# Clipped mixture of experts: the weighted sum moved from VectorE to ScalarE and GpSimd, the gate's product folded into silu

## The reference, cut to what matters

```python
def _swiglu(h):
    x_glu = jnp.minimum(h[..., ::2], LIMIT)              # LIMIT = 7.0
    x_lin = jnp.clip(h[..., 1::2], -LIMIT, LIMIT)
    return x_glu * jax.nn.sigmoid(ALPHA * x_glu) * (x_lin + 1.0)   # ALPHA = 1.702
...
logits = t @ gate_w + gate_b
top_v, top_i = jax.lax.top_k(logits, K)                  # K = 2
probs = jax.nn.softmax(top_v, axis=-1)
...
def body(acc, ew):
    w1, b1, w2, b2, we = ew
    h = _swiglu(t @ w1 + b1)
    y = h @ w2 + b2
    return (acc + we[:, None] * y, None)
```

## Time and profile before

| | us |
|---|---|
| median of 3 runs (lowest, highest) | 4638.23 (4637.52, 4643.8) |
| the profiled execution, its own time | 4647.3 |
| its span in the trace | 4644.3 |
| this sublayer in the trace, first VectorE instruction to the next sublayer's first matmul | 1157.0 to 1558.5 |
| TensorE busy over the span | 3836.4 (83%) |
| VectorE | 2840.3 (61%) |
| ScalarE | 2070.5 (45%) |
| GpSimd | 1152.7 (25%) |

### The profile page before, as it was taken

One profiled execution on the slowest core, in us unless ns is written; L12 is line 12 of the kernel. 1 busy time (PEld: TensorE's weight loads), 2 busy tenths in 40 slices (PEclk: granted clock), 3 DMA queues, 4 the chain that ended last, 5 costly groups with the idle time before them and its releaser, 6 DMA issues. The chain is left out here.

```text
span 4644.3 us, 84590 instructions
## 1 busy us (share of the span) xinstructions
PE 3836.4 (83%) x33378; PEld 2574.5 (55%) x33378; DVE 2840.3 (61%) x7587; ACT 2070.5 (45%) x3471; POOL 1152.7 (25%) x783
## 2 busy tenths in 40 slices
PE   0688888887999879898999996555359999598999
PEld 0466666566556556664555554435237776465665
DVE  9576777656899657666565655892452222476555
ACT  4466666544333225555554544430134444354332
POOL 3444444222444221003445452320000000010000
PEclk9999999999999769899999997776679999798999
DMA  2222222000000010000000000004100000000000
GB/s 92 47 47 47 50 48 48 17 1 1 1 1 1 1 51 2 2 1 1 2 2 2 2 2 1 21 21 153 59 14 1 1 1 1 28 2 2 1 10 10
DMA packets 58286, 92.04 MB, mean 20 GB/s; under 512 B 15922, under 2 KB 42501, under 8 KB 56133
## 3 DMA queue, kind: packets, MB, share of 16 engines
q1 hardware_dynamic: 53620, 79.83, 7.4%
q10 hardware_dynamic: 4272, 6.81, 0.4%
HBM read 42.43 MB, written 10.62 MB: 11 GB/s over the span
## 5 line engine op out<-in xcount | busy, mean ns | idle before, releaser
L853 PE MATMUL banks<-XT,weight_region 128*128 128x512 f32 x1696 | 781.2, 599 | 2.2 <-DVE T L1229 2.2
L875 PEld LDWEIGHTS banks<-weight_region,HT 128*128 128x128 f32 x4672 | 560.2, 192 | 151.4 <-issue 91.3
L1252 DVE SCALAR_TENSOR_TENSOR x_res<-banks,WT,x_res 128x128 f32<-128x128 f32 x1056 | 297.1, 344 | 488.7 <-PE banks L875 449.0
L875 PE MATMUL banks<-weight_region,HT 128*128 128x128 f32 x4672 | 569.6, 276 | 21.6 <-DVE HT L1240 15.3
L853 PEld LDWEIGHTS banks<-XT,weight_region 128*128 128x128 f32 x1696 | 305.8, 193 | 288.2 <-issue 283.2
L1005 ACT ACTIVATE HT<-banks,weight_region 128x512 f32<-128x512 f32 x256 | 173.4, 688 | 239.1 <-PE banks L853 232.9
L1068 POOL TENSOR_TENSOR FNM<-FNM,FRS 128x8 f32<-128x8 f32 x16 | 4.6, 288 | 1045.1 <-ACT FRS L964 1045.1
L458 DVE TENSOR_REDUCE MX<-banks 128x8 f32<-128x1152 f32 x128 | 173.2, 1353 | 116.0 <-PE banks L275 113.8
L384 ACT COPY PT<-banks 128x384 f32<-128x384 f32 x384 | 171.6, 481 | 132.1 <-PE banks L285 130.4
L1643 ACT COPY PT<-banks 77x512 f32<-77x512 f32 x256 | 143.3, 582 | 195.3 <-PE banks L1565 195.3
L1096 POOL TENSOR_TENSOR T<-T,T 128x512 f32<-128x512 f32 x128 | 162.8, 1273 | 210.8 <-ACT T L1028 208.3
(11 more groups left out here) (466 smaller groups left out, 8647.1 us busy)
## 6 DMA issues: line engine op xcount, KB each, us to landing
FL<-RAW SPq DMA_DIRECT2D x512, 64.0 KB, 2.3
T<-s4d_k_dram SPq DMA_DIRECT2D x8, 1024.0 KB, 5.8
weight_region<-in_l_ffn__w_dram SPq DMA_DIRECT2D x2, 2048.0 KB, 7.8
film_dram<-F SPq DMA_DIRECT2D x8, 512.0 KB, 2.9
weight_region<-in_l_ffn__w_dram ACTq DMA_DIRECT2D x2, 2048.0 KB
film_out<-film_dram SPq DMA_DIRECT2D x3, 1024.0 KB, 6.2
x_res<-in_x_dram SPq DMA_DIRECT2D x1, 2048.0 KB
weight_region<-in_l_ffn__w_dram SPq DMA_DIRECT2D x2, 1024.0 KB, 9.8
```

The costliest lines, as they stand in the source:

```text
L853: nc.tensor.matmul(PS[:, q % 4, :], w, xt, start=True, stop=True).then_inc(s.h_ps, 1)
L875: ins = nc.tensor.matmul(PS[:, 4 + u % 2, b * P:(b + 1) * P], HT[:, u % 2, j, b * P:(b + 1) * P], w2[j], start=j == 0, stop=j == len(w2) - 1)
L1252: ins = nc.vector.scalar_tensor_tensor(R[:, t, :], PS[:, 4 + u % 2, b * P:(b + 1) * P], WT[:, t, e:e + 1], R[:, t, :], ALU.mult, ALU.add)
```

## The change

For the kind "swiglu" alone:

- ScalarE computes silu(1.702 x), which is 1.702 x sigmoid(1.702 x), in place of sigmoid; T2 then holds 1.702 times the gate's product. The product on GpSimd (L1096) is gone, and `gate` reads T2.
- The factor 1/1.702 goes into the routing weights: a new small tile WS = WT / 1.702, one VectorE instruction per pair in `share`.
- `spill` becomes True: ScalarE scales down's result into a new tile T4 (`weigh`, four instructions per unit, with WS), and GpSimd adds it to the residual (`add_rows`, one instruction of 128x512 per unit). VectorE no longer runs `combine`. The second bias is copied to SBUF by ScalarE (`save_bias`) and added by GpSimd (`add_saved`), and VectorE no longer runs `add_bias`.
- Waits follow: hidden(u) waits for silu of the unit before, gate(u) for ScalarE, down(u) for `weigh` (of unit u-2) where it waited for `combine`, and the final statistics for GpSimd's sums.

```diff
-    spill = False
+    spill = kind == "swiglu"
...
-                        act.wait_ge(s.wt, g // 2 + 1)
+                        act.wait_ge(s.ws, g // 2 + 1)
...
-                                                   scale=WT[:, g * GB + b, e:e + 1])
+                                                   scale=WS[:, g * GB + b, e:e + 1])
...
-                                act.wait_ge(s.gs, k - 1)
-                            nc.scalar.activation(T2[:, k % 2, :], T1[:, k % 2, :], ACT.Sigmoid, scale=1.702).then_inc(s.sig, 1)
+                                act.wait_ge(s.gl2, k - 1)
+                            nc.scalar.activation(T2[:, k % 2, :], T1[:, k % 2, :], ACT.Silu, scale=SLOPE).then_inc(s.sig, 1)
...
-                    if kind == "swiglu":
-                        for j in range(2):
-                            q = 2 * u + j
-                            pool.wait_ge(s.sig, q + 1)
-                            nc.gpsimd.tensor_tensor(T1[:, q % 2, :], T1[:, q % 2, :], T2[:, q % 2, :], ALU.mult).then_inc(s.gs, 1)
...
+                    if spill:
+                        dve.wait_ge(s.wt, gp + 1)
+                        nc.vector.tensor_scalar(WS[:, gp * PB:(gp + 1) * PB, :], wt, 1.0 / SLOPE, None, ALU.mult).then_inc(s.ws, 1)
...
                             if k >= 2:
+                                dve.wait_ge(s.sig, k - 1)
                                 dve.wait_ge(s.gl2, k - 1)
...
-                        dve.wait_ge(s.gs, k + 1)
+                        dve.wait_ge(s.sig, k + 1)
                         dve.wait_ge(s.dve_h, k + 1)
-                        nc.vector.scalar_tensor_tensor(HT[:, u % 2, j, :], T3[:, k % 2, :], -6.0, T1[:, k % 2, :],
+                        nc.vector.scalar_tensor_tensor(HT[:, u % 2, j, :], T3[:, k % 2, :], -6.0, T2[:, k % 2, :],
```

More of the change, by code:

```diff
@@ L706 @@
 NEG = -1.0e30
+SLOPE = 1.702
 def moe(nc, E, kind, prefetch=(), store=None):
@@ L753, in moe @@
                       "selx den rden wt wt_ps wtT_ps wtT b2_ps accb b1 "
-                      "xo xo2 w_ld st h_ps act_done dve_h glu sig gs gl2 y_ps yw acc badd f_st rm_var2 f_var f_ln f_rs f_nm gate1 gate2") as (s, ctx):
+                      "xo xo2 w_ld st h_ps act_done dve_h glu sig gl2 y_ps yw acc badd f_st rm_var2 f_var f_ln f_rs f_nm gate1 gate2 ws") as (s, ctx):
         sb = E.scratch(ctx)
@@ L761, in moe @@
         XS = sb("XS", [P, PB, NE]); EX = sb("EX", [P, PB, NE]); SEL = sb("SEL", [P, PB, NE]); SX = sb("SX", [P, PB, NE])
-        DEN = sb("DEN", [P, PB]); WT = sb("WT", [P, NB, NL]); WTT = sb("WTT", [NE, 2, GT])
+        DEN = sb("DEN", [P, PB]); WT = sb("WT", [P, NB, NL]); WS = sb("WS", [P, NB, NL]) if spill else None; WTT = sb("WTT", [NE, 2, GT])
         GATE = sb("GATE", [P, PB]) if shared else None; GL = sb("GL", [P, PB]) if shared else None
```

## The result

| | before | after |
|---|---|---|
| median of 5 runs (lowest, highest), us | 4641.65 (4637.52, 4643.8) | 4616.9 (4608.03, 4622.48) |
| span of the profiled execution, us | 4644.3 | 4615.0 |

The ratio is 0.9947, with a 95% interval of 0.9933 to 0.9962: faster by 18 to 31 us of 4642.

What follows compares the result with a forecast made beforehand. The prediction took TensorE's floor of 5.22 us per unit as the bound, with VectorE's full list adding waits. Body 20.0, head 0.15 and tail 2.4 made 22.6 us off 4638.2: 4616 us, range 4609 to 4629.

Steps and rivals of the forecast that it cites:

- What binds: In the changed sublayer, TensorE's floor is 5.22 us per plain unit; VectorE needs 5.05 and is late where it has extra work.
- Body: From up(2) to up(63): floor 337.6 of 358.1 us, 20.5 lost to VectorE, 20.0 taken as gain.
- the restart of the array: TensorE between up(2) and up(63): of 20.5 us lost, 15.3 are named waits, the rest the array's restart behind them.
- VectorE's thin slack: VectorE's gates in busy units: they still fit before down, by 0.7 us at k = 3 and 1.0 at k = 14.
- the walk: Step-by-step timing after up: gate ends at 8.0 at k = 3; for unit 6, silu at 7.7 and gate at 8.6.
- the half case: Rival: gates at k = 13 to 15 still late (7.5 us), statistics' stalls partly kept (2.5): 4626 us; chance 0.15.
- when VectorE's gate is over: GpSimd's sum beside a plain unit runs 1.6 to 2.9 into the next, after VectorE's gate, which ends 0.5 into it.
- ScalarE: Four added scalings per unit take 1.28 us (1.1 to 1.7), silu is free; 2.4 of 5.22, no one waits in plain units.
- Head: First units: hidden(1) and up(2) start 0.65 us earlier, but 0.5 of unit 1's stall stays; net gain 0.15.
- Tail: From up(63) to the last norm's root: 14.61 us before, 12.2 after; gain 2.4.
- no change: Rival: saved time lost to the clock afterwards, or a new wait for weigh or T4 in each unit: 4636 us; chance 0.10.
- The slower one: Rival: GpSimd's sums meet VectorE's gates in every unit, a pair of gates costs 2.98 us: 4651 us; chance 0.07.

Runs made afterwards that it cites:

- spare instructions: Full change plus two or four SBUF-to-SBUF instructions of 128x512 per unit on VectorE behind the gate: 4629.87 us with two, 4654.92 us with four.
- the repeat: The full change run once more, with nothing altered: 4617.73 us, ratio 0.9948 against the kernel before.

## Why the prediction was right, point by point

- **What binds.** TensorE's floor of 5.22 us per unit held: after the change it stands at nearly every plain unit, and the windows show TensorE without idle time. VectorE's list as the cause of the 19 waits is shown by three runs: silu alone leaves them all, and spare instructions bring 10 and 19 waits back. VectorE's share came to 84%, where near 80% was expected.
- **Body.** 20.0 less 0.5 was expected, 18.7 came. The term that was too large is TensorE's floor, which I had made too short: the unit with the bias takes 7.39, not 5.22 + 1.98 = 7.20, and other extras have seams of 0.08. Four times 0.19, three seams of 0.08 behind the logits and 0.05 at k = 4 in three pairs come to 1.15, of which the prediction had taken off 0.5. With the stall left at unit 1, 0.62 against 0.5, that makes the 0.8 missing. So of the 5.2 us that the prediction put down to the restart of the array, about 1 was TensorE's own time. What can be read of a restart is that a down ran 2.05 behind a wait and 1.95 without one, under 2 us for 19 waits; the rest was not traced.
- **VectorE's thin slack.** At k = 3 the gate was to end 8.0 after its up, with 8.66 as the limit. It ended at 8.55, and the walk had missed why: the gate at 1284.11, read below, took 2.35, as the sum of GpSimd lay on it. TensorE had its matmuls ready at 8.66, and down ran 2.00 for 1.95. The margin of 0.7 was used up to 0.1, and the half case was nearer than I had said. That step, "when VectorE's gate is over", holds in plain units and fails where VectorE is late.

```profile
1284.11 2.35 DVE L1240 SCALAR_TENSOR_TENSOR HT<-T,T 128x512 f32<-128x512 f32 x2
1284.55 1.36 POOL L1081 TENSOR_TENSOR x_res<-x_res,T 128x512 f32<-128x512 f32 x1 [3.60 <-ACT T L983]
...
1286.52 1.86 PEld L876 LDWEIGHTS banks<-weight_region,HT 128*128 128x128 f32 x16 [0.62 <-DVE HT L1240]
1286.57 2.00 PE L876 MATMUL banks<-weight_region,HT 128*128 128x128 f32 x16
```

- **ScalarE.** Four scalings took 1.12 to 1.14, not 1.28, near the lower bound of 1.1. One silu took 631 ns in the mean and one sigmoid 632, so it was free. At k = 5 of the second pair silu(22) was done 7.4 after up(22) and the gate 8.2, for 7.7 and 8.6 in the walk; down was reached at 10.7. No wait of TensorE or VectorE is put down to a scaling; only GpSimd's sum waits for it.
- **Head.** up(2) came 0.65 nearer to up(0), the number worked out, and a part of that is luck. up(1) to up(2), which the change shortens, gained 0.77, and up(0) to up(1) lost 0.12 by its clock. In the repeat the whole head gained 1.15.
- **Tail.** The root at 12.03 for 12.2; 2.58 for 2.4.
- **Rivals.** *Half* and *no change* did not come: no down waits for the gate at k = 3 or 14, and none for a scaling. The slower one named the right mechanism, contention of GpSimd's sum with VectorE's gates. Its place was wrong: it is not the length of VectorE's unit that it decides, but a ring through GpSimd. That ring is the sum without silu, and there it cost 33 us. In the full change the ring is cut, and the rule of the Trainium skill (GPSIMD Engine Reference, Key points) on shared interfaces, with which the trace agrees once more (0.69 to 1.73 per gate, 2.58 to 3.12 for two products), has only lone gates to act on, at k = 3 and 4 (2.35 and 2.36 per pair of gates in the second pair of groups).
- **Outside.** Of the 24.7 us between the medians 21.9 is the sublayer. The forecast of 4616 and the median of 4616.9 agree better than the steps do, and that is luck: the median of before proved to be 4641.65, 3.4 above the 4638.23 that the forecast starts from, and 21.9 off it gives 4619.8. The 2.8 us between that and 4616.9 lie outside the sublayer, where lengths change from run to run.

## What to carry to other kernels

Take the time of a unit on each engine apart from its latency around the ring: moving work off the engine that is full helps only if no engine in the ring receives it at a bad moment. Two parts of a change may be worth nothing and a loss when done alone and gain together (here silu alone gained 2 us in the trace of the sublayer, the sum alone lost 33 us of the median, and both together gained 25), so a part is judged in the schedule in which it will stand. Where GpSimd and VectorE both work in SBUF, look at what lies beside what; holding GpSimd's sum back until the gate was done was worth 50 us here (4675.04 to 4625.22).

## What the hardware showed that I had not expected

- GpSimd suffers as well from VectorE's instructions of one SBUF input. The sum of 128x512 took 1.27 alone, 1.33 in the mean of the full change, and 2.18 in the mean beside four spare SBUF-to-SBUF instructions per unit; group from 1189 to 1520 us:

```profile
L1082 POOL TENSOR_TENSOR x_res<-x_res,T 128x512 f32<-128x512 f32 x54 | 117.5, 2176 | 220.1 <-ACT T L984 219.7 <-POOL x_res L1088 0.3
```

- Clips of the same size that read PSUM neither slow GpSimd nor are slowed by it: 0.73 to 0.76 each in the runs, with GpSimd's sum at 1.27 and its two products at 2.59 beside them.
- Two additions on GpSimd whose two inputs are the same tile took 2.04 us, and two products of different tiles 2.58. One addition of different tiles took 1.27, so the inputs, and not the operation, look like the cause; no run separates them.
- The next sublayer's length varied between 150.3 and 156.8 us with the same code, in steps of about 5 us per quarter that ran at a granted clock of 0.54 and not 0.73.
